# Two-layer cross-attention on one core: moving half of the gram rows, the second layer's values and the image tokens' products into the first two score steps

## The reference

```python
# layer 0: 77 text tokens and 435 image tokens, each with its own softmax
out = attend(q, k, v) + attend(q, k_ip, v_ip)
x = out @ Wo.T + bo + x
# layer 1: 508 text tokens and 4 image tokens
probs_t = softmax(q @ k_t.T * scale)            # text
text_out = probs_t @ v_t
qsem = l2norm(probs_t @ text_ehs)               # 512 channels per head and token
sem = qsem @ l2norm(ip_ehs).T
probs_ip = softmax(q @ k_ip.T * scale + 0.5 * sem) * spatial_mask
x = (text_out + probs_ip @ v_ip) @ W_out + b_out + x
```

## Time and profile before

| | |
|---|---|
| median of 3 runs | 1808.93 us |
| lowest and highest | 1806.72 and 1810.32 us |
| the profiled execution | 1810.82 us |
| its span, first to last instruction | 1809.0 us |
| mean granted TensorE clock | 0.960 of 2.4 GHz |

### The profile page before, as it was taken

How to read it: one execution, slowest core, us unless ns; L and a number is a source line. 1 busy time by engine, 2 the same in 40 slices (tenths; PEclk the granted TensorE clock), 3 DMA queues, 4 the chain that set the end, 5 groups by cost and what they waited for, 6 DMA issues and landing times.

```text
span 1809.0 us, 34075 instructions
## 1 busy us (share of the span) xinstructions
PE 1635.4 (90%) x8608; PEld 1234.2 (68%) x8608; DVE 1272.7 (70%) x3548; ACT 1116.1 (62%) x2323; POOL 463.6 (26%) x1225
## 2 busy tenths in 40 slices
PE   5788989999978898999988888999998889999993
PEld 2455469999445447999835544999974554799991
DVE  2487358887678717888758853788875883588875
ACT  1599157776279627777429943677734991577760
POOL 0244013232025302323104411222301540233220
PEclk9899989999989998999989999999998999899996
DMA  7210220000301031001030111100012102100000
GB/s 234 75 35 22 88 65 21 19 18 20 114 29 35 13 104 53 22 17 32 1 121 31 35 48 61 59 20 17 28 45 85 35 26 79 36 18 21 17 20 15
DMA packets 47284, 83.04 MB, mean 46 GB/s; under 512 B 4417, under 2 KB 11857, under 8 KB 47185
## 3 DMA queue, kind: packets, MB, share of 16 engines
q1 hardware_dynamic: 43040, 74.15, 12.5%
q10 hardware_dynamic: 4144, 7.76, 1.4%
HBM read 47.78 MB, written 34.10 MB: 45 GB/s over the span
## 4 chain that ended last, share of the span: by engine, by line
PE 77%; ACT 10%; issue 5%; DVE 5%; DMA 1%; POOL 1%; ACTq 1%; SPq 0%; POOLq 0%; DVEq 0%
PE ps_w L838 37%; PE ps_s L838 17%; PE ps_t L838 16%; PE ps_b L838 4%; ACT probsT_high L461 4%; ACT probsT L469 4%; DVE row_max L648 2%; PE ps_m L838 2%; ACT q_slot L454 1%; ACT probs L495 1%; POOL probsT_low L383 1%; ACT probs L478 0%; ACT probs L536 0%; DMA w_ki<-in_wki 0%; DVE row_max L679 0%
## 5 line engine op out<-in xcount | busy, mean ns | idle before, releaser
L637 DVE TENSOR_TENSOR probsT_low<-probsT,probsT_high 128x512 fp32r<-128x512 f32 x560 | 394.1, 704 | 85.2 <-ACT probsT L469 76.0
L461 ACT ACTIVATE probsT_high<-ps_t 128x512 fp32r<-128x512 f32 x640 | 382.6, 598 | 113.9 <-PE ps_t L838 109.9
L838 PE MATMUL ps_w<-gram,probsT_high 128*128 128x416 f32 (+2 forms) x1280 | 390.8, 316 | 0.0
L469 ACT ACTIVATE probsT<-ps_t 128x512 f32<-128x512 f32 x640 | 384.0, 600 | 0.0
L838 PE MATMUL ps_w<-gram_low,probsT_high 128*128 128x384 f32 (+2 forms) x1280 | 354.5, 305 | 0.0
L495 ACT ACTIVATE probs<-ps_s,exp_bias 128x508 f32<-128x508 f32 x320 | 220.9, 691 | 125.9 <-POOL exp_bias L394 82.6
L838 PE MATMUL ps_s<-k_slot,q_slot 96*128 96x512 f32 x640 | 249.6, 434 | 32.0 <-issue 13.0
L838 PE MATMUL ps_t<-q_slot,k_slot 98*128 98x512 f32 x640 | 266.1, 435 | 11.0 <-ACT q_slot L454 9.2
L394 POOL TENSOR_SCALAR exp_bias<-row_max 128x1 f32<-128x1 f32 x320 | 129.7, 405 | 551.8 <-DVE row_max L679 551.8
L838 PEld LDWEIGHTS ps_w<-gram_low,probsT_high 128*128 128x128 f32 (+1 forms) x1280 | 244.8, 191 | 11.1
L838 PEld LDWEIGHTS ps_w<-gram,probsT_high 128*128 128x128 f32 (+1 forms) x1280 | 243.2, 190 | 11.5
(11 more groups left out here) (153 smaller groups left out, 2056.9 us busy)
## 6 DMA issues: line engine op xcount, KB each, us to landing
q_slot<-parts_q SPq DMA_DIRECT2D x160, 96.0 KB
k_slot<-parts_k SPq DMA_DIRECT2D x160, 96.0 KB
parts_k<-probsT_high SPq DMA_DIRECT2D x24, 512.0 KB, 4.2
parts_q<-probsT_low SPq DMA_DIRECT2D x24, 512.0 KB, 4.3
parts_k<-probsT_high SPq DMA_DIRECT2D x24, 128.0 KB, 3.8
parts_q<-probsT_low SPq DMA_DIRECT2D x24, 128.0 KB, 3.6
ctx_sb<-in_ctxT ACTq DMA_DIRECT2D x3, 1024.0 KB, 8.3
vip_rep<-vip_rows SPq DMA_DIRECT2D x16, 160.0 KB, 3.6
```

The source lines that it names most:

```text
L461: nc.scalar.activation(probsT_high[1 - par][:, t, :], ps_t[:, t % 2, :], ACT.Exp, scale=SCALE)
L469: nc.scalar.activation(probsT[:, t, :], ps_t[:, t % 2, :], ACT.Exp, scale=SCALE).then_inc(pt_block[l], 1)
L637: nc.vector.tensor_tensor(probsT_low[1 - par][:, t, :], probsT[:, t, :], probsT_high[1 - par][:, t, :].bitcast(F32), ALU.subtract).then_in ...
L838: return nc.tensor.matmul(out, lhsT, rhs, start=start, stop=stop)
```

## The change

Nothing is added to or taken from what is computed; eight of the ten jobs after `q1` are made elsewhere.

- **TensorE.** Only `g` 0 and 1 stay behind `q1`. Step -2 now makes scores 0 and 1 of head 0, `g` 2, scores 2 and 3, `g` 3, `v1` 0. Step -1 makes `v1` 1, 2 and 3 behind the scores 0, 1 and 2 of head 1, and `ipn` and `vip` behind the last. The wait for all `v1` before the first scores is gone.
- **Banks.** All ten jobs go round three banks (`late_ring`: `ps_w` 0, `ps_w` 1, `ps_b`), and `free_bank` waits for the job three places earlier.
- **ACT.** `gram_rows` 2 stands between the first two and the last two `exps` of step -2, `gram_rows` 3 and `v1` 0 at its end; `v1` 1 to 3 stand in step -1, behind `exps` 0, `exps` 1 and `expT` 2.
- **DVE.** The low parts of gram rows 2 and 3 move to step -2 (`gram_lows`), `ip_context` to the end of step -1.
- **POOL.** The gram's second copy and the heads' values of heads 0 and 1 (`values_of`) move from ahead of and inside steps -2 and -1 to behind them (`gram_ready`).

```diff
+LATE = [("g", i) for i in range(TB)] + [("v1", t) for t in range(TB)] + [("ipn", 0), ("vip", 0)]
...
-        late = {("ipn", 0): ps_b[:, :], ("vip", 0): ps_w[0][:, :]}
+        late_ring = [ps_w[0][:, :], ps_w[1][:, :], ps_b[:, :]]
+        late = {job: late_ring[i % len(late_ring)] for i, job in enumerate(LATE)}
...
+            def values_of(b, head, par):
+
+                src = v1_sb[:, :, :].rearrange("p t (h d) -> p t h d", d=D)[:, :, head, :]
+                nc.gpsimd.tensor_copy(gram[par][:, :, GA:GV], src).then_inc(v_high, 1)
+                pool.wait_ge(v_high, HEADS * b + head + 1)
+                pool.sem_inc(passed, 1)
+                nc.gpsimd.tensor_tensor(gram[par][:, :, GV:GW], src, gram[par][:, :, GA:GV].bitcast(F32), ALU.subtract)\
+                    .then_inc(v_in, 1)
...
+                if use and scores:
+                    values_of(b, n + 2, par)
...
-                wait_freed(pool, b, "g", TB - 1)
...
-                run_heads(step1, pool, b)
+                def gram_ready():
+
+                    wait_freed(pool, b, "g", TB - 1)
+                    pool.sem_inc(passed, 1)
+                    for i in range(TB):
+                        lo = P * max(i, 1) - P
+                        last = nc.gpsimd.tensor_copy(gram[1][:, i, lo:GA], gram[0][:, i, lo:GA])
+                    last.then_inc(gram_copied, 1)
+                    wait_freed(pool, b, "v1", TB - 1)
+                    pool.sem_inc(passed, 1)
+                    values_of(b, 0, 0)
+                    values_of(b, 1, 1)
+
+                run_heads(step1, pool, b, gram_ready)
...
+                first, second = not use and not transposed, not use and transposed
...
+                    if second and c < TB - 1:
+                        v1_rows(b, c + 1)
+                if first:
+                    gram_rows(b, 2)
                 if scores:
                     exps(2)
                     exps(3)
+                if first:
+                    gram_rows(b, 3)
+                    v1_rows(b, 0)
...
-                    if not use and not transposed and c == 1:
-                        ip_context(b)
+                    if not use and not transposed and c % 2 == 1:
+                        gram_lows(b, 2 + c // 2)
...
+                if not use and transposed:
+                    ip_context(b)
...
+                if (name, m) in late:
+                    i = LATE.index((name, m))
+                    if i >= len(late_ring):
+                        wait_freed(pe, b, *LATE[i - len(late_ring)])
...
                 by_channels(b, "q1", "q1", x1_sb)
-                for i in range(TB):
-                    over_e(free_bank(b, "g", i)[:, 0:T - P * i], lambda e: ctx_sb[:, e, P * i:P * i + P],
-                           lambda e: ctx_sb[:, e, P * i:T]).then_inc(job_done, 1)
-                by_keys(b, "v1", "v1")
-
-                wait_freed(pe, b, "v1", TB - 1)
+                gram_of_context(b, 0)
+                gram_of_context(b, 1)
```

More of the change, by code:

```diff
@@ L546, in batch @@
                 highs(b, "q1")
[L547 to L551, removed]
+                gram_rows(b, 0)
+                gram_rows(b, 1)
                 def context_done():
@@ L710, in step1, with gram_lows @@
                         lowT(b, 1, n, par, c)
+                if not use and transposed:
+                    ip_context(b)
+            def gram_lows(b, i):
+                wait_job(dve, b, "g", i)
+                dve.wait_ge(gram_high, TB * b + i + 1)
+                src = bank("g", i)
+                diag = P if i < TB - 1 else P - IPN
+                if i > 0:
+                    cols = slice(P * (i - 1), P * (i - 1) + diag)
+                    nc.vector.tensor_tensor(gram_low[:, i, cols], src[:, 0:diag], gram[0][:, i, cols].bitcast(F32), ALU.subtract)
+                cols = slice(P * i - P + diag, GA)
+                nc.vector.scalar_tensor_tensor(out=gram_low[:, i, cols], in0=src[:, diag:T - P * i], scalar=2.0,
+                                               in1=gram[0][:, i, cols].bitcast(F32), op0=ALU.mult, op1=ALU.subtract)\
+                    .then_inc(freed["D"], 1)
             def ip_context(b):
@@ L746, in batch @@
                 lows(b, "q1")
-                for i in range(TB):
-                    wait_job(dve, b, "g", i)
-                    dve.wait_ge(gram_high, TB * b + i + 1)
-                    src = bank("g", i)
-                    diag = P if i < TB - 1 else P - IPN
-                    if i > 0:
-                        cols = slice(P * (i - 1), P * (i - 1) + diag)
-                        nc.vector.tensor_tensor(gram_low[:, i, cols], src[:, 0:diag], gram[0][:, i, cols].bitcast(F32), ALU.subtract)
-                    cols = slice(P * i - P + diag, GA)
-                    nc.vector.scalar_tensor_tensor(out=gram_low[:, i, cols], in0=src[:, diag:T - P * i], scalar=2.0,
-                                                   in1=gram[0][:, i, cols].bitcast(F32), op0=ALU.mult, op1=ALU.subtract)\
-                        .then_inc(freed["D"], 1)
+                gram_lows(b, 0)
+                gram_lows(b, 1)
                 run_heads(step1, dve, b)
@@ L990, in step1 @@
                     scoresT_of(1, g, k, 0)
+                first, second = not use and not transposed, not use and transposed
                 if scores:
                     scores_of(0)
+                if second:
+                    by_keys(b, "v1", "v1", 1)
                 if use:
@@ L998, in step1 @@
                     scores_of(1)
-                if not use and not transposed:
-                    ip_context(b)
+                if first:
+                    gram_of_context(b, 2)
+                if second:
+                    by_keys(b, "v1", "v1", 2)
                 if use:
@@ L1006, in step1 @@
                     scores_of(2)
+                if second:
+                    by_keys(b, "v1", "v1", 3)
                 if transposed:
@@ L1010, in step1 @@
                     scores_of(3)
+                if first:
+                    gram_of_context(b, 3)
+                    by_keys(b, "v1", "v1", 0)
+                if second:
+                    ip_context(b)
                 if use:
@@ L1050, in for_layer0 @@
                        lambda e: w_big["v0"][:, e, :]).then_inc(job_done, 1)
-                by_keys(b, "v0i", "vi0")
+                for t in range(TB):
+                    by_keys(b, "v0i", "vi0", t)
             def transposed_heads(b, name, l):
```

32 lines of the change are left out of this document (12 added, 20 removed).

## The result

| | median | lowest to highest | profiled execution | its span |
|---|---|---|---|---|
| before | 1808.25 us (4 runs) | 1806.72 to 1810.32 | 1810.82 | 1809.0 |
| after | 1818.15 us (4 runs) | 1817.73 to 1821.12 | 1817.73 | 1815.9 |

The ratio is 1.0058, 95% interval 1.0045 to 1.0071: the changed kernel is 9.9 us slower. The forecast was 1826, so the direction held, the range (1815 to 1836) held, and the point was 8 us too high.

A forecast was written before the change was run, and what follows sets the result against it. TensorE, 90% busy, was taken to bound the kernel, with slot 0's DMA setting layer 1's first scores. Growth 25.7 less 8.55 for the earlier start plus 0 for dips gave +17.2 us: 1826, range 1815 to 1836.

The forecast's parts named there:

- What bounds the start: Before layer 1's first scores: slot 0's DMA lands 4.94 us after issue, so TensorE idles 9 to 10.5 us per batch.
- C: Slot 0 lands sooner than 4.94 us after its issue: 1821 at 3.6 us, 1816 at 2.5 us; chance 0.12.
- E: Opening steps close up fully and slot 0 lands in 2.5 us: 1798 us; chance 0.03.
- The gain from the earlier start: With work ahead of the scores taken away, they start once slot 0 is in: 8.55 us gained over four batches.
- Half clock behind the wait: TensorE runs the first 5 us after slot 0 at half clock, since the clock falls while it idles.
- Growth of the opening: From first scores to head 1's transposed scores, 6.1 + 6.15 + 6.15 + 7.3 = 25.7 us longer over four batches.
- The dips: Clock dips behind the opening cost 1.8 us each; one in four batches taken, as now: 0 us.
- rival B: The clock comes back at 6.8 instead of 5.1 us and dips in all batches: 1835 us; chance 0.17.
- Rival D: The opening steps close up fully, first product ending at 21.6 us, -0.3 us per batch: 1808 us; chance 0.05.

The follow-up runs named there:

- warm: The changed kernel plus nine unread 128x512 products per batch on TensorE in the idle time before slot 0: 1816.09 us, ratio 1.0042 to the kernel before.
- warm_copy: The changed kernel with nine unread products before slot 0 and POOL's gram copy between its two opening steps: 1810.99 us, ratio 1.0015.
- block_between: `ip_front` with POOL's values of heads 0 and 1 ahead of the sums and the second block of values in step -2's gap: 1794.63 us, ratio 0.9931.
- ip_front: The changed kernel with gram rows 2, 3, first block of values, ipn, vip ahead of the scores, POOL's copy ahead of its steps: 1808.84 us, ratio 1.0007.
- one_block: The kernel before with only the last block of values moved into step -2, ipn and vip behind later scores: 1806.08 us, ratio 0.9999.
- cover_warm: The changed kernel with gram rows 2, 3 and the first block of values ahead of the scores, then four unread products: 1814.77 us, ratio 1.0037.
- issues_sooner: `block_between` with ACT issuing vip's store and the next batch's x loads ahead of step -2: 1793.65 us, ratio 0.9930.

## Why the prediction was right, and where its sum was off

- **What bounds the start: right.** TensorE idles 8.82 to 8.90 us before the first scores in all four batches, released by the load; slot 0 came 4.8 us after its issue (229.43 - 224.62) against 4.94 of the earlier trace rows. Rivals C and E, an earlier slot, fell. The Trainium skill, "DMA: Bandwidth & Descriptors", section "Anatomy of one DMA", would have it in 2.2 us (an estimate for 96 KB), by a fit for DMAs issued from GpSimd, while SyncE issues these; the trace disagrees again. The wait itself was forecast at 9 to 10.5 us and is 8.9.
- **The gain from the earlier start: mis-sized, 8.55 forecast, 11.8 measured.** The step took the loads' issue times from one execution, and two of the four had been late ones (20.2 and 20.7 us behind q1 instead of 19.1). These don't move the kernel before, which comes to slot 0 at 26.9 either way, so its own trace gave no sign; they make 2.7 of the 3.2 us, the landing the rest. What varied there is the store's landing: the first load was issued 3.75 to 5.37 us behind the store.
- **Half clock behind the wait: right in kind, 3.6 to 3.9 us in three batches and some 6 in the second, instead of 5.** Row 2 took 3.27 us, forecast 3.5 (3.62 in the second batch, whose opening is a microsecond longer than the others). Its price was too high: "some 2 us per batch less" with the clock up is 1.2 in `warm` (4.9 us in the four stretches), and 2 us in all four batches together in the medians.
- **Growth of the opening: 25.0 us, forecast 25.7.** By batch 5.6, 6.7, 5.6 and 7.1. In three batches the steps held within 0.8 us: head 0's transposed scores at 9.0 to 9.2 (forecast 9.7), first products at 23.5 to 23.7 (23.9), head 1's transposed scores at 25.3 to 25.5 (25.7 to 25.9). POOL's copy ended at 21.9 in the first batch (forecast 22.65), and TensorE waited 1.72 us for it. ACT's shift, which the forecast had end level with TensorE at 25.8, was done at 24.6 (253.39 + 0.59) and held nothing up. That the second batch missed by 0.6 the other way brought the sum nearer to the forecast, which is luck.
- **The dips: 0 forecast, -1.8 measured against the first trace of before.** None of the changed kernel's four openings was followed by one, although the wait is 1.7 us. Before showed one in each of its two traces, in different batches. Taking "one in four, as now" was a guess about chance, and so was rival B, which fell. What brings a dip on isn't shown: in the two traces of before it followed waits of 1.57 and 1.95 us at the shift and not those of 1.49 and less, and the changed kernel's waits of 1.60 to 1.72 us, ahead of the first full step, brought none.
- **The rest.** 17.2 forecast; less 3.2 for the start, 0.7 for the growth and 1.8 for the dip leave 11.5, and the medians differ by 9.9. The 1.6 left is of the size of the flips named above (1.8 us each), and of the 0.7 by which before's median moved. Which of them it was can't be told. All of these terms were forecast on the slow side, and none of the misses is the earlier slot that the low end of the range was made for; that 1818 lies within it is owed to that width as much as to the working.
- **Rival D, the steps close up: fell.** With all of the moved work in the steps, the clock up and POOL's copy off the path (`warm_copy`), head 1's transposed scores still came at 23.6 us, 2 us behind D's 21.6, and TensorE still waited 1.0 to 1.1 us for vip, one of the jobs that the prediction named against D. The 19.0 to 20.8 us of `block_between` are no test of D, since its steps hold three blocks of values and none of the other moved jobs.

## What to carry to other kernels

Work ahead of a wait for a DMA is free up to the length of the wait: see how long the engine idles with nothing ahead of it (here 8.9 us), put just that much of its own work there (8.0 in `ip_front`, which left 0.6 to 0.9 idle), and only move the rest. What stands there beyond it puts off the start (26.9 us instead of 24.0), but taking just that away gains nothing by itself, as `one_block` shows. Of what is moved, the order decides: the version that beat both kernels had POOL's copy, its values and the image tokens' products off the end of the opening, and a block of values in a gap into which the clock was still up; the same block behind that gap paid the lower clock.

## What the runs showed of the hardware

- In `cover_warm` the granted clock stood at 1.00 until 230 and at 0.50 from 231 on, inside a step in which TensorE had little to do (0.32 busy in 230:231); filling the wait ahead of that step did not help the work behind it.
- In one and the same place of the program the same product takes 3.62 or 5.32 us, or 6.00 or 7.80 to 8.40, from one execution to the next. The two traces of the kernel before differ by 3.8 us in span by such flips and the like.
- Four DMA issues on ACT's queue took 2.75 us from the first one to the next activation (250.64 to 253.39 in the trace of after) and held up nothing there; three issues less made some 0.8 us in four batches of `issues_sooner`, and nothing that could be told in the time.
